# Weighted sum of a windowed attention written transposed with v stationary, probabilities normalised on GpSimd

## The chip, the cores and the metric

The kernel runs on one core of one Trainium2 chip. Its engines each run their own instruction stream and meet at semaphores: TensorE (PE in the rows; PEld is its weight load), VectorE (DVE), ScalarE (ACT), GpSimd (POOL), and SyncE (SP), which here only issues DMAs. The metric is the device time of one execution in microseconds (us). The profiled execution is one run with the hardware profiler on; its rows give times in us from the start of its span, and mean durations in ns.

## What is computed

Four residual steps on x of 4 x 512 x 128 in float32: a gated linear attention, a block of windowed-attention and MLP layers, a state-space (Mamba) layer, and the same windowed block again. Only the two windowed blocks are touched. One of their six layers is, cut to what matters:

```python
def local_attention(q, k, v):            # 16 heads of 64, windows of 32 tokens
    bk2, bv2 = look(bk), look(bv)        # each window sees itself and the one before: 64 keys
    sim = jnp.einsum('bhwie,bhwje->bhwij', bq, bk2) * QK_SCALE
    sim = jnp.where(mask, -jnp.finfo(sim.dtype).max, sim)
    attn = jax.nn.softmax(sim, -1)
    out = jnp.einsum('bhwij,bhwje->bhwie', attn, bv2)
    return out.reshape(b, h, n, d)

for i in range(6):
    x = attn_layer(shift_tokens(x), Wqkv[i], q_scale[i], k_scale[i], Wo[i]) + x
    x = ffn_layer(shift_tokens(x), ln_g[i], ln_b[i], W1[i], b1[i], W2[i], b2[i]) + x
```

attn_layer projects x to q, k and v, normalises and rotates q and k, calls local_attention and multiplies the result by Wo. ffn_layer is a LayerNorm, two up projections, a GELU and a down projection.

## The kernel before

Each windowed block is 24 iterations (6 layers x 4 batches), and each iteration handles the 512 tokens of one batch as four tiles of 128 tokens. The body of tile u (u = 0 to 3, called body u below) is written out by hand on every engine, in pe_body, act_body, dve_body and the loop over pool_rotate, and this hand-written order is the order of the work: no engine leaves it, each waits at its next semaphore. Two blocks of 24 iterations make 48 iterations and 192 bodies. Most iterations run in a hardware loop whose branch stands between body 3 and body 0.

The work is pipelined over tiles. Body u projects tile u+2 (pe_proj, six chunks of 512 columns into two PSUM banks in turn: chunks 0 to 3 are q and k, 4 and 5 are v), transposes q and k of tile u+1 and makes its scores (pe_qk_t, pe_scores), and transposes the probabilities of tile u and multiplies them with v (pe_probs_t, pe_pv). Between these stands a slice of the MLP of the batch before: in body 0 the Wo product (pe_wo, 2 x 8 matmuls), in body 1 the centring and variance (pe_center, pe_var), in body 2 the spread of 1/std (pe_rstd, L393) and the first up projection (pe_up, L405 and L406), in body 3 the other two up projections and the down projection.

PSUM has eight banks: proj_ps (2), tr_ps (2, all transposes), s_ps (2, scores), o_ps (2, weighted sum and MLP). The path of one tile from scores to Wo before the change:

- ScalarE: act_exp_odd (8 activations with sums, L556) and act_exp_even (L563) write the unnormalised probabilities m["p"]. DVE: dve_den sums the even heads (L732) and takes the reciprocal (L736) of all 16 sums.
- TensorE: pe_probs_t (L315) transposes m["p"] into tr_ps, ScalarE copies it out (act_probs_t, L546). pe_pv (L348) then multiplies: for each of 8 head pairs, 2 parities and 4 windows, one matmul with a 64 x 32 block of transposed probabilities as stationary operand and 64 columns of v as moving operand. A float32 matmul is two records in the trace, so a half of pe_pv is 32 matmuls and 64 records. The result stands as tokens x channels in o_ps.
- DVE: dve_out (L743) multiplies o_ps by the reciprocals into m["o"]. One body later TensorE transposes m["o"] (pe_out_t, L285, 8 transposes) into tr_ps, and ScalarE copies it to m["ot"] (act_out_t, L528), from which pe_wo reads.

GpSimd in body u adds the rotated halves of q and k of tile u+2 (L895, one for each of four chunks, each after DVE's product L686), then refines the inverse norms (L882 to L885) and scales the four chunks (L901). ScalarE squares the chunks (L510) and copies v to m["v"] (L518). SyncE then issues 16 DMAs per tile that spread v over m["vp"] (sp_pairs); for tile u+2 they wait until the weighted sum of tile u is done (o_mm), and act_v of the next body waits for them to land.

## Time and profile before

| | us |
|---|---|
| median of 3 runs | 4693.23 |
| lowest, highest | 4692.45, 4695.45 |
| profiled execution | 4693.35 |
| its span, first to last instruction | 4691.5 |

Mean granted TensorE clock in the profiled execution: 0.918 of full speed. The profiled execution lies 0.1 us from the median and 1.9 us above its own span. A busy TensorE is not one at its peak, since matmuls overlap and their ends are modelled; what a group of matmuls costs is therefore read from the distance between the start of the first row and the start of the next one.

### The profile page before, as it was taken

Reading aid. Unit: us, or ns where it says so; the run is one execution under the profiler, and the core shown is the slowest. Engines: PE = TensorE matmul, PEld = TensorE weight load, DVE = VectorE, ACT = ScalarE, POOL = GpSimd, SP = SyncE. Lnnn points to the kernel's source line nnn. Section 1 sums busy time; section 2 is a strip of 40 time slices with the busy share of each in tenths; the row PEclk is TensorE's granted clock in tenths of the full one; section 3 lists DMA queues with packets and bytes.
Section 4 is the critical chain, followed back from the end, with each engine's and each line's share of the span. In section 5 each row is a group of like instructions: output and inputs, shape, how many; then the busy total and the mean of one; then the engine's idle time right before and its main releaser. Section 6 shows DMA issues by size and latency. Waiting matters only on the chain. (4 is left out here: it accounts for less than half of the span.)

```text
span 4691.5 us, 161781 instructions
## 1 busy us (share of the span) xinstructions
PE 3817.1 (81%) x62204; PEld 2454.2 (52%) x62204; DVE 3473.8 (74%) x5422; ACT 2716.9 (58%) x6885; POOL 2274.0 (48%) x2468
## 2 busy tenths in 40 slices
PE   7788888888888888885655688888888888888887
PEld 2465555555555555552111265655656565565654
DVE  7677777777777777764888777777777777777774
ACT  2466566666656666662333366665666666566663
POOL 3455545554555555440444565555555555555551
PEclk9899999999999999996677799999999999999998
DMA  1222222222222222220000022222222222222221
GB/s 33 57 75 74 72 74 68 71 72 73 74 71 74 67 74 70 73 71 13 0 0 0 21 69 72 73 75 69 73 73 70 69 75 74 68 75 72 70 69 47
DMA packets 243984, 290.20 MB, mean 62 GB/s; under 512 B 60750, under 2 KB 131014, under 8 KB 243142
## 3 DMA queue, kind: packets, MB, share of 16 engines
q1 hardware_dynamic: 243262, 279.62, 23.2%
q8 instruction: 569, 9.32, 0.9%
q14 instruction: 153, 1.25, 0.1%
HBM read 77.03 MB, written 1.05 MB: 17 GB/s over the span
## 5 line engine op out<-in xcount | busy, mean ns | idle before, releaser
L895 POOL TENSOR_TENSOR qk_rows<-rot_products 128x512 f32<-128x512 f32 x768 | 982.3, 1279 | 1601.2 <-DVE rot_products L686 1601.2
L686 DVE TENSOR_TENSOR rot_products<-psum,rot_scaled 128x1024 f32<-128x1024 f32 x768 | 936.5, 1219 | 319.4 <-ACT squares L510 270.3
L271 PE MATMUL psum<-wqkv_hi,xs_hi 128*128 (+1 forms) x1152 | 618.7, 537 | 234.7 <-ACT v_rows L518 85.8
L901 POOL TENSOR_TENSOR qk_rows<-qk_rows,rnorm 128x512 f32<-128x512 f32 x768 | 801.7, 1074 | 15.0
L518 ACT ACTIVATE v_rows<-psum 128x512 f32<-128x512 f32 x384 | 223.8, 597 | 899.1 <-PE psum L273 681.6
L299 PE MATMUL psum<-ident,qk_rows 128*128 128x128 f32 x3072 | 508.1, 318 | 240.1 <-issue 152.8
L510 ACT ACTIVATE squares<-psum 128x512 f32<-128x512 f32 x768 | 481.3, 627 | 223.0 <-PE psum L273 187.6
L299 PEld LDWEIGHTS psum<-ident,qk_rows 128*128 128x128 f32 x3072 | 413.0, 163 | 364.1 <-issue 329.4
L688 DVE TENSOR_REDUCE sumsq<-squares 128x8 f32<-128x512 f32 x768 | 519.1, 676 | 0.0
L743 DVE TENSOR_TENSOR o_rows<-psum,rden 128x512 f32<-128x512 f32 x384 | 247.8, 686 | 309.6 <-PE psum L348 304.9
L272 PE MATMUL psum<-wqkv_lo,xs_hi 128*128 (+1 forms) x1152 | 474.2, 412 | 0.0
L273 PE MATMUL psum<-wqkv_hi,xs_lo 128*128 (+1 forms) x1152 | 474.1, 412 | 0.0
L556 ACT ACTIVATE probs<-psum,minus_row_max 128x64 f32<-128x64 f32 x1536 | 458.7, 328 | 13.8 <-DVE minus_row_max L720 12.2
L271 PEld LDWEIGHTS psum<-wqkv_hi,xs_hi 128*128 128x128 f32 x1152 | 233.5, 203 | 350.5 <-issue 302.7
L1410 POOL TENSOR_TENSOR mb_hc<-mb_h,mb_c 128x512 f32<-128x512 f32 x128 | 211.4, 1670 | 354.4 <-DVE mb_h L1379 337.4
L348 PE MATMUL psum<-v_pairs,probs_t 64*32 64x64 f32 x24576 | 355.4, 228 | 27.5 <-issue 20.6
L348 PEld LDWEIGHTS psum<-v_pairs,probs_t 64*32 64x32 f32 x24576 | 279.9, 107 | 180.3 <-issue 179.1
L371 PE MATMUL psum<-o_t,wo 128*128 128x512 f32 x768 | 352.4, 602 | 11.1 <-issue 10.7
L334 PEld LDWEIGHTS psum<-k_t,q_t 64*32 64x32 f32 x24576 | 269.7, 105 | 151.6 <-issue 150.9
L556 ACT ACTIVATION_READ_ACCUMULATOR probs<-psum,minus_row_max 128x1 f32 x1536 | 338.6, 220 | 0.0
L334 PE MATMUL psum<-k_t,q_t 64*32 64x64 f32 x24576 | 332.6, 224 | 2.6 <-issue 2.6
L546 ACT ACTIVATE probs_t<-psum 128x512 f32<-128x512 f32 x384 | 207.2, 594 | 168.1 <-PE psum L315 168.0
(161 smaller groups left out, 6653.4 us busy)
## 6 DMA issues: line engine op xcount, KB each, us to landing
v_pairs<-v_rows SPq DMA_DIRECT2D x3072, 64.0 KB, 2.0
wo<-in_Wo SPq DMA_DIRECT2D x48, 512.0 KB, 4.0
wqkv_staged<-in_Wqkv SPq DMA_DIRECT2D x52, 384.0 KB, 3.2
w<-in_W SPq DMA_DIRECT2D x48, 341.0 KB, 3.1
w<-in_W SPq DMA_DIRECT2D x48, 128.0 KB
w<-in_W SPq DMA_DIRECT2D x48, 42.5 KB
qk_scale<-in_qk_scale SPq DMA_DIRECT2D x12, 128.0 KB, 3.3
rot_base<-in_rot SPq DMA_DIRECT2D x2, 512.0 KB, 3.7
```

Of the source, the lines that this page charges most:

```text
L271: nc.tensor.matmul(proj_ps[c % 2], xh, wh, start=True, stop=False)
L272: nc.tensor.matmul(proj_ps[c % 2], xh, wl, start=False, stop=False)
L273: nc.tensor.matmul(proj_ps[c % 2], xl, wh, start=False, stop=True).then_inc(S["qkv_mm"], 1)
L299: last = nc.tensor.transpose(tr_ps[g % 2][:, i * P:(i + 1) * P], m["qk"][:, u % 2, (4 * g + i) * P:(4 * g + i + 1) * P], ident[:, :])
L334: last = nc.tensor.matmul(s_ps[par][WIN * w:WIN * w + WIN, 64 * hp:64 * hp + 64], m["qt"][rows, hp, WIN * w:WIN * w + WIN], m["kt"][rows, ...
L348: last = nc.tensor.matmul(o_ps[par][WIN * w:WIN * w + WIN, 64 * hp:64 * hp + 64], m["pt"][rows, hp, WIN * w:WIN * w + WIN], m["vp"][rows, ...
L510: nc.scalar.activation(m["sq"][:, c % 2, :], proj_ps[c % 2], ACT.Square).then_inc(S["sq_done"], 1)
L556: last = nc.scalar.activation(m["p"][:, hp, 1, :], s_ps[1][:, 2 * WIN * hp:2 * WIN * (hp + 1)], ACT.Exp, bias=m["mx"][:, 1, hp:hp + 1], ac ...
L686: V.tensor_tensor(m["mm"][:, c % 2, :, :].rearrange("p a (h e) -> p a h e", e=DH), ps, cos_sin, ALU.mult)\
L688: V.tensor_reduce(m["ss"][:, HC * c:HC * c + HC], m["sq"][:, c % 2, :].rearrange("p (h e) -> p h e", e=DH), AX.X, ALU.add)\
L895: G.tensor_tensor(qk[:, c * CH:(c + 1) * CH].rearrange(half, a=2, e=DH // 2), cos, sin[:, :, ::-1, :], ALU.add)\
L901: G.tensor_tensor(part, part, m["rn"][:, u % 2, HC * c:HC * c + HC].unsqueeze(2) .to_broadcast([P, HC, DH]), ALU.mult).then_inc(S["rot_don ...
```

## The change

The matmul of the weighted sum swaps its operands: v (64 x 64) is stationary, the transposed probabilities (32 columns) are moving, and the result comes out as channels x tokens, as pe_wo wants it. The transposes of m["o"] go, with m["o"] itself. A reciprocal belongs to a token and a head, which now lie along the columns of o_ps, so the normalisation moves ahead of the transpose of the probabilities: GpSimd multiplies m["p"] by the reciprocals (pool_probs, two instructions of 128 x 512) after the add of chunk 1, and pe_probs_t waits for it (pn_done). DVE's dve_out goes. ScalarE copies o_ps straight to m["ot"], at the end of body u instead of in the middle of body u+1. The matmuls run over windows, then over two neighbouring head pairs (j, which picks the half of the array's columns), then over parity (which picks the half of its rows); their number stays. Everything that waited for o_ps to be read by DVE (o_ev) now waits for ScalarE's copies (oT_ev). The rows of Wo are permuted on the host to match.

```diff
-        def pe_out_t(it, u, qk_after):
-
-            for g in range(2):
-                nc.tensor.wait_ge(S["o_ev"], cnt(it, 2, u, 2))
-                if qk_after:
-                    nc.tensor.wait_ge(S["qkT_ev"], cnt(it, 4, u + 2, g + 3))
-                else:
-                    nc.tensor.wait_ge(S["pT_ev"], cnt(it, 2, u, g + 1))
-                for i in range(4):
-                    hp = 4 * g + i
-                    last = nc.tensor.transpose(tr_ps[g][:, i * P:(i + 1) * P],
-                                               m["o"][:, hp, :, :].rearrange("p a e -> p (a e)"),
-                                               ident[:, :])
-                last.then_inc(S["oT_mm"], 1)
...
-        def pe_probs_t(it, u, qk_after, out_before):
+        def pe_probs_t(it, u, qk_after):
 
             for g in range(2):
-                nc.tensor.wait_ge(S["exp0_done"], cnt(it, 1, u, 1))
-                nc.tensor.wait_ge(S["exp1_done"], cnt(it, 1, u, 1))
-                if out_before:
-                    nc.tensor.wait_ge(S["oT_ev"], cnt(it, 2, u - 1, g + 1))
-                elif qk_after:
+                nc.tensor.wait_ge(S["pn_done"], cnt(it, 2, u, 2))
+                if qk_after:
                     nc.tensor.wait_ge(S["qkT_ev"], cnt(it, 4, u + 1, g + 3))
+                else:
+                    wait(nc.tensor, S["pT_ev"], cnt(it, 2, u - 1, g + 1))
...
-            for hp in range(4 * half, 4 * half + 4):
-                for par in range(2):
-                    rows = slice(64 * par, 64 * par + 64)
-                    for w in range(WPT):
-                        last = nc.tensor.matmul(
-                            o_ps[par][WIN * w:WIN * w + WIN, 64 * hp:64 * hp + 64],
-                            m["pt"][rows, hp, WIN * w:WIN * w + WIN],
-                            m["vp"][rows, u % 2, w, DH * hp:DH * hp + DH],
-                            start=True, stop=True)
-                    if hp == HP - 1:
-                        last.then_inc(S["o_mm"], 1)
+            for hp in range(4 * half, 4 * half + 4, 2):
+                for w in range(WPT):
+                    for j in range(2):
+                        for par in range(2):
+                            rows = slice(64 * par, 64 * par + 64)
+                            last = nc.tensor.matmul(
+                                o_ps[par][64 * j:64 * j + 64, P * (hp // 2) + WIN * w:P * (hp // 2) + WIN * w + WIN],
+                                m["vp"][rows, u % 2, w, DH * (hp + j):DH * (hp + j) + DH],
+                                m["pt"][rows, hp + j, WIN * w:WIN * w + WIN],
+                                start=True, stop=True)
+                            if half == 1 and hp == 6 and w == WPT - 1 and j == 1:
+                                last.then_inc(S["o_mm"], 1)
...
-            wait(nc.tensor, S["o_ev"], cnt(it, 2, u))
+            wait(nc.tensor, S["oT_ev"], cnt(it, 2, u))
...
-                if prev:
-                    pe_out_t(it, u - 1, nxt)
...
-                pe_probs_t(it, u, nxt, prev)
+                pe_probs_t(it, u, nxt)
...
         def act_out_t(it, u):
             t = u % TILES
+            nc.scalar.wait_ge(S["o_mm"], cnt(it, 2, u, 2))
+            if t == 0:
+                wait(nc.scalar, S["d1_mm"], it + u // TILES)
             for g in range(2):
-                nc.scalar.wait_ge(S["oT_mm"], cnt(it, 2, u, g + 1))
-                if t == 0:
-                    wait(nc.scalar, S["d1_mm"], it + u // TILES)
                 nc.scalar.activation(m["ot"][:, 4 * g:4 * g + 4, t * P:(t + 1) * P],
-                                     tr_ps[g].rearrange("p (i q) -> p i q", i=4), ACT.Copy).then_inc(S["oT_ev"], 1)
+                                     o_ps[g].rearrange("p (i q) -> p i q", i=4), ACT.Copy).then_inc(S["oT_ev"], 1)
...
                     act_square(it, u + 3, 0)
                 if nxt:
                     act_exp_even(it, u + 1)
+                act_out_t(it, u)
...
-        def dve_out(it, u):
-            V.wait_ge(S["den_done"], cnt(it, 1, u, 1))
-            for g in range(2):
-                V.wait_ge(S["o_mm"], cnt(it, 2, u, g + 1))
-                wait(V, S["oT_mm"], cnt(it, 2, u))
-                V.tensor_tensor(m["o"][:, :, g, :], o_ps[g].rearrange("p (h e) -> p h e", e=DH),
-                                m["rden"][:, u % 2, g, :].unsqueeze(2).to_broadcast([P, 8, DH]),
-                                ALU.mult).then_inc(S["o_ev"], 1)
...
+        def pool_probs(it, u):
+            G.wait_ge(S["den_done"], cnt(it, 1, u, 1))
+            for par in range(2):
+                p = m["p"][:, :, par, :]
+                G.tensor_tensor(p, p, m["rden"][:, u % 2, par, :].unsqueeze(2).to_broadcast([P, HP, 2 * WIN]), ALU.mult).then_inc(S["pn_done"], 1)
+
+        def pool_rotate(it, u, norm=False):
             qk = m["qk"][:, u % 2, :]
             wait(G, S["qkT_mm"], cnt(it, 4, u - 1))
...
+                if norm and c == 1:
+                    pool_probs(it, u - 2)
```

Three places show what the edits do to the order. In the first, TensorE in body 2, the rows run from after the second chunk of the projection to the transposes of the probabilities (L285 is pe_out_t, L271 to L273 are one chunk of the projection, L405 and L406 the up projection, L315 the transposes of the probabilities). Before:

```order
L285 MATMUL psum<-ident,o_rows 128x128 [waits qkT_ev,o_ev]
L285 MATMUL psum<-ident,o_rows 128x128 x3
...
L271 MATMUL psum<-wqkv_hi,xs_hi 128x512 [waits m_done,sq_done]
L272 MATMUL psum<-wqkv_lo,xs_hi 128x512
L273 MATMUL psum<-wqkv_hi,xs_lo 128x512
L405 MATMUL psum<-xn_mlp,w 128x512 [waits xn2,w1_in,o_ev]
L406 MATMUL psum<-xn_mlp,w 128x512
L315 MATMUL psum<-ident,probs 128x128 [waits oT_ev,exp1_done,exp0_done]
L315 MATMUL psum<-ident,probs 128x128 x3
```

The same place in the changed kernel:

```order
L270 MATMUL psum<-wqkv_hi,xs_hi 128x512 [waits m_done,sq_done]
L271 MATMUL psum<-wqkv_lo,xs_hi 128x512
L272 MATMUL psum<-wqkv_hi,xs_lo 128x512
L388 MATMUL psum<-xn_mlp,w 128x512 [waits xn2,w1_in,oT_ev]
L389 MATMUL psum<-xn_mlp,w 128x512
L298 MATMUL psum<-ident,probs 128x128 [waits qkT_ev,pn_done]
L298 MATMUL psum<-ident,probs 128x128 x3
```

Eight transposes are gone, and those of the probabilities wait for GpSimd (pn_done) in place of ScalarE's exponentials. The second place is ScalarE from the end of body 1 to the middle of body 2 (L563 is act_exp_even, L539 copies q and k out of tr_ps, L510 squares a chunk, L528 is act_out_t). Before:

```order
L563 ACTIVATE probs<-probs 128x8x64 [waits sub_done]
L539 ACTIVATE q_t<-psum 128x512 [waits qkT_mm,s_mm]
L539 ACTIVATE q_t<-psum 128x512 [waits qkT_mm]
L510 ACTIVATE squares<-psum 128x512 [waits red_done,qkv_mm]
L539 ACTIVATE k_t<-psum 128x4x128 [waits qkT_mm,s_mm]
L539 ACTIVATE k_t<-psum 128x4x128 [waits qkT_mm]
L510 ACTIVATE squares<-psum 128x512 [waits red_done,qkv_mm]
L528 ACTIVATE o_t<-psum 128x4x128 [waits oT_mm] x2
L510 ACTIVATE squares<-psum 128x512 [waits red_done,qkv_mm]
```

The same place in the changed kernel:

```order
L543 ACTIVATE probs<-probs 128x8x64 [waits sub_done]
L508 ACTIVATE o_t<-psum 128x4x128 [waits o_mm]
L508 ACTIVATE o_t<-psum 128x4x128
L519 ACTIVATE q_t<-psum 128x512 [waits qkT_mm,s_mm]
L519 ACTIVATE q_t<-psum 128x512 [waits qkT_mm]
L490 ACTIVATE squares<-psum 128x512 [waits red_done,qkv_mm]
L519 ACTIVATE k_t<-psum 128x4x128 [waits qkT_mm,s_mm]
L519 ACTIVATE k_t<-psum 128x4x128 [waits qkT_mm]
L490 ACTIVATE squares<-psum 128x512 [waits red_done,qkv_mm] x2
```

The two copies to m["ot"] moved ahead of the copies of q. The third place is GpSimd in every body. Before, the four adds of the rotation follow each other:

```order
L895 TENSOR_TENSOR qk_rows<-rot_products 128x512 [waits m_done]
L891 REGISTER_ALU
L895 TENSOR_TENSOR qk_rows<-rot_products 128x512 [waits m_done]
L880 REGISTER_ALU
L882 TENSOR_TENSOR newton_t<-newton_y 128x32 [waits rot_done,seed]
```

In the changed kernel the multiplies stand between the second add and the third:

```order
L869 TENSOR_TENSOR qk_rows<-rot_products 128x512 [waits m_done]
L856 REGISTER_ALU
L859 TENSOR_TENSOR probs<-probs,rden 128x8x64 [waits den_done]
L859 TENSOR_TENSOR probs<-probs,rden 128x8x64
L865 REGISTER_ALU
L869 TENSOR_TENSOR qk_rows<-rot_products 128x512 [waits m_done]
```

GpSimd now waits in its stream for DVE's reciprocals (den_done), with the adds of chunks 2 and 3 queued behind.

## Rows read from the trace of the kernel before

**Rows 1.** The page: busy time and share of the span of each engine.

```profile
PE 3817.1 (81%) x62204; PEld 2454.2 (52%) x62204; DVE 3473.8 (74%) x5422; ACT 2716.9 (58%) x6885; POOL 2274.0 (48%) x2468
```

**Rows 2.** Busy time of the engines in bodies 1, 2, 3, 0: PE, PEld, DVE, ACT, POOL; clock.

```profile
1000.92:1016.30 15.38, 13.84 (x326) 10.62 (x319) 14.10 (x24) 11.77 (x24) 8.57 (x10) 1.00 0.29 71
1016.30:1035.42 19.12, 16.51 (x321) 11.56 (x315) 14.55 (x25) 14.18 (x38) 10.01 (x13) 0.91 0.32 84
1035.42:1060.63 25.21, 18.55 (x327) 11.70 (x323) 18.76 (x30) 16.96 (x51) 12.30 (x15) 1.00 0.20 50
1060.63:1082.99 22.36, 20.97 (x325) 13.80 (x325) 14.30 (x24) 9.51 (x28) 11.40 (x12) 0.92 0.33 85
```

**Rows 3.** TensorE's waits in 1002 to 1330 (four iterations): total us, times, longest.

```profile
PE psum L299 <- issue: 14.5, 4, 3.8
PE psum L299 <- ACT q_t L539: 7.5, 4, 2.3
```

**Rows 4.** ScalarE, timeline of bodies 1, 2: start, us, instruction, [idle before, releaser].

```profile
1013.83 1.09 ACT L518 ACTIVATE v_rows<-psum 128x512 f32<-128x512 f32 x2 [3.10 <-DMA v_pairs<-v_rows]
...
1019.56 1.13 ACT L539 ACTIVATE q_t<-psum 128x512 f32<-128x512 f32 x2
...
1025.24 1.08 ACT L528 ACTIVATE o_t<-psum 128x512 f32<-128x512 f32 x2
```

**Rows 5.** TensorE, timeline of body 2.

```profile
1020.35 1.94 PE L299 MATMUL psum<-ident,qk_rows 128*128 128x128 f32 x8 [2.25 <-ACT q_t L539]
...
1024.47 1.03 PE L285 MATMUL psum<-ident,o_rows 128*128 128x128 f32 x8
1025.26 0.48 PE L271 MATMUL psum<-wqkv_hi,xs_hi 128*128 x1
...
1027.76 1.04 PE L315 MATMUL psum<-ident,probs 128*128 128x128 f32 x8
```

**Rows 6.** DVE, timeline: the reciprocals in bodies 2, 3 and 0.

```profile
1026.05 0.25 DVE L736 RECIPROCAL rden<-den 128x16 f32<-128x16 f32 x1
...
1043.28 0.25 DVE L736 RECIPROCAL rden<-den 128x16 f32<-128x16 f32 x1
...
1066.66 0.25 DVE L736 RECIPROCAL rden<-den 128x16 f32<-128x16 f32 x1
```

**Rows 7.** GpSimd: a group of the page, and the timeline of body 2.

```profile
L895 POOL TENSOR_TENSOR qk_rows<-rot_products 128x512 f32<-128x512 f32 x768 | 982.3, 1279 | 1601.2 <-DVE rot_products L686 1601.2
...
1033.55 4.05 POOL L901 TENSOR_TENSOR qk_rows<-qk_rows,rnorm 128x512 f32<-128x512 f32 x4
```

**Rows 8.** Timeline of body 3, on DVE and TensorE.

```profile
1041.90 0.75 DVE L780 SCALAR_TENSOR_TENSOR hidden<-psum,layer_vectors,gelu 128x512 f32<-128x512 f32 x1 [0.18 <-ACT gelu L588]
...
1042.50 1.12 PE L285 MATMUL psum<-ident,o_rows 128*128 128x128 f32 x8 [1.64 <-ACT k_t L539]
...
1045.87 1.03 PE L315 MATMUL psum<-ident,probs 128*128 128x128 f32 x8
```

**Rows 9.** TensorE, timeline of body 0: first half of Wo, then the probabilities.

```profile
1067.41 3.67 PE L371 MATMUL psum<-o_t,wo 128*128 128x512 f32 x8 [0.22 <-issue]
1070.92 1.04 PE L315 MATMUL psum<-ident,probs 128*128 128x128 f32 x8
```

**Rows 10.** Weight loads by line, and two stretches of TensorE's timeline.

```profile
L348 PEld LDWEIGHTS psum<-v_pairs,probs_t 64*32 64x32 f32 x24576 | 279.9, 107 | 180.3 <-issue 179.1
L371 PEld LDWEIGHTS psum<-o_t,wo 128*128 128x128 f32 x768 | 143.2, 191 | 175.8 <-issue 171.9
...
1006.62 0.95 PE L385 MATMUL psum<-mean,hidden 128*128 128x1 f32 x8
...
1034.63 0.86 PE L348 MATMUL psum<-v_pairs,probs_t 64*32 64x64 f32 x64
```

**Rows 11.** The end of the last iteration: DVE's dve_out, then Wo.

```profile
4637.78 1.29 DVE L743 TENSOR_TENSOR o_rows<-psum,rden 128x512 f32<-128x512 f32 x2 [1.65 <-issue]
...
4641.83 1.19 PE L371 MATMUL psum<-o_t,wo 128*128 128x512 f32 x1 [0.73 <-issue]
```

More of the change, by code:

```diff
@@ L376, in pe_center @@
         def pe_center(e, o_free):
-            wait(nc.tensor, S["o_ev"], o_free)
+            wait(nc.tensor, S["oT_ev"], o_free)
             nc.tensor.wait_ge(S["d1_ev"], e + 1)
@@ L381, in pe_var @@
         def pe_var(e, o_free):
-            wait(nc.tensor, S["o_ev"], o_free)
+            wait(nc.tensor, S["oT_ev"], o_free)
             nc.tensor.wait_ge(S["xc_ev"], 2 * (e + 1))
@@ L389, in pe_rstd @@
         def pe_rstd(e, o_free):
-            wait(nc.tensor, S["o_ev"], o_free)
+            wait(nc.tensor, S["oT_ev"], o_free)
             nc.tensor.wait_ge(S["diag_done"], e + 1)
@@ L396, in pe_up @@
             if j < 2:
-                wait(nc.tensor, S["o_ev"], o_free)
+                wait(nc.tensor, S["oT_ev"], o_free)
             if j == 0:
@@ L494, in pe_ffn @@
             pe_body(last, True, False)
-            pe_out_t(last, 3, False)
             pe_wo(last, 0)
@@ L644, in act_ffn @@
             act_body(last, True, False)
-            act_out_t(last, 3)
             act_center(last)
@@ L827, in dve_body @@
                     dve_rstd(it - 1)
-                dve_out(it, u)
         def dve_weights(it):
@@ L910, in pool_ffn @@
                 for u in range(TILES):
-                    pool_rotate(it, u + 2)
+                    pool_rotate(it, u + 2, True)
             for u in range(2):
-                pool_rotate(last, u + 2)
+                pool_rotate(last, u + 2, True)
+            for u in range(2, TILES):
+                pool_probs(last, u)
         SP = nc.sync
@@ L1570, in layout @@
          "W2": f["L0_ffn_W2"]}
+    heads = [4 * i + 2 * j + par for par in range(2) for i in range(4) for j in range(2)]
+    r["Wo"] = r["Wo"].reshape(DEPTH, HEADS, DH, D)[:, heads].reshape(DEPTH, INNER, D)
     qs, ks = f["L0_ffn_q_scale"], f["L0_ffn_k_scale"]
```

15 lines of the change are left out of this document (5 added, 10 removed).

## Prediction

> **What bounds the kernel now.** Read the shares first. TensorE is busy 81% of the span, DVE 74%, ScalarE 58%, GpSimd 48% [rows 1], and in one iteration of 82.07 us, bodies 1, 2, 3 and 0, TensorE is busy 69.87, the sum of its column [rows 2]. TensorE is the nearest to a bound, but 12 us of an iteration are not its work, so the second view is what it waits for. Its longest waits are 3.6 us at the loop's branch and 1.9 us for ScalarE's copy of q at the start of body 2, each once per iteration [rows 3]. So the kernel changes its bound within one iteration, and I walk through it body by body.
>
> Body 1 hangs on the DMAs of v: ScalarE stands still 3.10 us until they land and only then, at 1013.83, copies v [rows 4]. From there it has no gap: exponentials, a chunk, exponentials, and the copies of q at 1019.56. TensorE, idle since before, gets its bank back at 1020.35 [rows 5]. Those DMAs start when the weighted sum of body 0 is done, so body 1 has about 3 us in which TensorE and GpSimd may be late at no cost. From the probabilities of body 2 on, TensorE paces itself to the end of that body. At the start of body 3 ScalarE is the late one again: its GELU releases DVE at 1041.90, and TensorE waits 1.64 us for the copy of k queued behind that GELU [rows 8]. After the probabilities of body 3, and through body 0, TensorE sets the time.
>
> **The change, part by part.** The profiled execution took 4693.35 us, 0.1 from the median, so the sum is made against 4693.4. Stretches are counted from the start of one row to the start of the next.
>
> *Transposes of the weighted sum.* Eight transposes advance TensorE by 1025.26 - 1024.47 = 0.79 us [rows 5]. That is saved only where TensorE sets the time: in body 0, where also the 0.22 us before Wo go [rows 9], since the copies that Wo needs are then made a body earlier. Together -1.0. In bodies 1, 2 and 3 something else arrives later, as follows.
>
> *ScalarE's copies to m["ot"].* The two copies take 1.08 us [rows 4], before and after, but they move from the middle of a body, where ScalarE often waits, to just ahead of the copies of q. At the end of body 1 ScalarE has no gap, so the copies of q and the transposes of k behind them come 1.1 us later: TensorE's wait of 2.25 us [rows 5] grows. At the end of body 2 it is the same, since ScalarE works without a gap from the copy of v to the GELU [rows 8]: again +1.1. At the end of body 3 the loop's branch (3.6 us) hides it, at the end of body 0 the 3 us of body 1 do.
>
> *DVE's dve_out.* Two instructions less per body. DVE only waits longer for ScalarE's squares instead, so nothing is gained on the path. Should DVE have been the late one, up to 1.3 us per body would come back.
>
> *GpSimd's multiplies.* No row has this form. The nearest are the scaling by rnorm, 4.05 us for four, 1.01 each, and the rotation's add with a reversed operand, 1.28 [rows 7]. I take 1.05, as the scaling is the same operation with the same broadcast: 2.1 us a body (2.0 to 2.6). They start when the reciprocals are there and TensorE follows. A handover between engines shows as 0.18 us [rows 8]; I count 0.3 for both. GpSimd has the time: it is busy at most 12.30 us of any body [rows 2]. The question is when they end, against TensorE's present start of the transposes of the probabilities:
> - Body 2: reciprocals end at 1026.30 [rows 6], multiplies at 1028.4, TensorE could start at 1028.7. It starts at 1027.76 now [rows 5]. So +0.9, on top of the 1.1 by which this whole chain is already late.
> - Body 3: 1043.53 [rows 6] + 2.4 = 1045.9 against 1045.87 [rows 8]: nothing beyond the 1.1. The 1.64 us and the 0.79 us that TensorE saves here are used up in waiting.
> - Body 0: 1066.91 [rows 6] + 2.4 = 1069.3 against 1070.92 - 1.0 = 1069.9 [rows 9]: hidden, with 0.6 us to spare.
> - Body 1: late by 1 to 2 us, hidden by the wait for the DMAs.
>
> Behind the waiting multiplies stand the adds of chunks 2 and 3. They wait for DVE's third product anyway, which comes only after the reciprocals, so they lose under a microsecond, and GpSimd's next wait, for DVE's seeds of the inverse norms, takes it up.
>
> *The weighted sum itself.* Still 64 records per half, 0.86 us now [rows 10]. The moving side halves from 64 to 32 columns; the stationary side doubles from 32 to 64. A load of 32 columns lasts 107 ns, one of 128 columns 191 [rows 10], so a column costs 0.88 ns and 64 columns occupy their part of the array for 56 ns. The variance stretch shows what a stream looks like that is bound by loads: 8 loads of 128 columns in 0.95 us, some 0.1 each [rows 10]. Today's 64 loads of 32 columns would take 64 x 28 ns = 1.8 us one after another, and the half takes 0.86, so at least two to three of them run at once. After the change there are four independent quarters. If all four load at once, a half needs 64 x 56 / 4 = 0.9 us plus the last matmul: I take +0.2 per half. If only 2.5 do, 1.4 us, +0.6. Below: if streaming alone set the pace, half the columns could save up to 0.2 per half. So +0.4 per body (-0.4 to +1.2). It counts in bodies 3 and 0, +0.8; in body 2 ScalarE's 1.1 cover it up to 1.1, in body 1 the DMAs do.
>
> The Trainium skill has a rule against this very swap. TensorEngine Tiling (Array Packing), section Instruction Overhead: each matmul carries some 60 cycles, one of 1 column takes as long as one of 60, and a tiling factor should not be taken from a dimension that is already small. By it 64 records of 32 columns cannot pass faster than 25 ns apart, 1.6 us a half, and the time would be near 4940 (+1.5 per body: 2 x 1.5 in bodies 3 and 0 and 0.4 in body 2, on 2.1 from the other terms). By the rows the sum keeps its +0.2: they have 64 records of 64 columns in 0.86 us, 13 ns apart, already below that floor.
>
> *Sum.* Per iteration 1.1 + 0.9 + 1.1 - 1.0 + 0.8 = +2.9 us. Two iterations of the 48 are first ones without MLP, so 46 x 2.9 = +133. At the end of a block the change helps: from dve_out at 4637.78 to Wo at 4641.83 are 4.05 us [rows 11], of which only ScalarE's two copies and a handover, about 1.4, remain. Twice -2.6 is -5. 4693.4 + 133 - 5 = **4821 us**, slower by 2.7%. With the ends of the weighted sum (-0.8 and -0.8 more, or +1.6 and a little) this case spans 1.3 to 4.7 us per iteration: 4748 to 4905.
>
> **The rivals.**
> - *The late waits are hidden, and TensorE's work decides.* Then each body saves 0.79 and pays 0.4, body 3 loses its 1.64 and body 0 its 0.22: -3.4 per iteration, 48 x 3.4 = 163, **4530 us**. For it: TensorE is the busiest engine. It decides if the reciprocals of bodies 2 and 3 come more than 2 us earlier than now, say because DVE without dve_out is ahead. Against it: the squares and the copies of q, not DVE, gate them. 0.12.
> - *The weight loads bind.* Two to three at once: 1.4 us per half, +4.7 per iteration, **4904 us**. It shows as a half of more than 1.2 us. For it: nothing in the rows shows four loads at once with certainty. The skill's rule above ends here too. 0.15.
> - *The clock.* In bodies 2 and 0, which start with TensorE's long waits, the granted clock is 0.91 and 0.92 on average, in the other two it is 1.00 [rows 2]. The change adds idle stretches of 1 to 2 us ahead of the probabilities in bodies 1, 2 and 3. If one of them per iteration brings a further stretch at 1.2 instead of 2.4 GHz of the kind that body 2 has now (9% of 19.12 us, doubled: 3.4 us at half speed, 1.7 lost), that is +1.7 per iteration, **4899 us**. Against it: the 1.64 us wait in body 3 leaves that body at 1.00. 0.13.
> - *Both effects are half as large* and the result is within 0.2% of now: 0.05.
>
> **How the numbers follow.** My case 0.55, faster 0.12, loads 0.15, clock 0.13, no change 0.05. The likeliest is my case, 4821 us. The range must leave out at most 0.2: it drops the faster rival and the ends, and takes 4730 to 4930. Slower by over 0.2% (about what a measurement of this kernel tells from none): 0.55 + 0.15 + 0.13 = 0.83; same 0.05; faster 0.12.
>
> **What would show it.** Right: TensorE's wait for the copy of q in body 2 grows from 2.25 to about 3.3 us; the probabilities' transposes wait for GpSimd in bodies 1, 2 and 3, and not in body 0; the idle before the projection's chunk 0 in body 1 stays bound to the DMAs; a half of the weighted sum lasts 1.0 to 1.1 us. Wrong: no wait for GpSimd in body 2 (then the first rival), a half at or below 0.86 us, an iteration under 82 us, or a mean clock well under 0.918.

## The result, and the profile after

| | before | after |
|---|---|---|
| median, us (lowest to highest of 4 runs) | 4694.34 (4692.45 to 4695.82) | 5002.71 (5002.20 to 5005.41) |
| ratio to before, 95% interval | | 1.0658 (1.0640 to 1.0677) |
| profiled execution: time, span, us | 4693.35, 4691.5 | 5002.95, 5000.5 |

The change makes the kernel 6.6% slower. The forecast was 2.7% slower, 4821 us, with a range to 4930: the sign was right, and of the loss of 308 us it had 128. The span and mean granted clock of after:

```profile
core 0: 5000.5 us, clock 0.892
```

Its page, busy time and share of each engine:

```profile
PE 3891.9 (78%) x60668; PEld 2452.9 (49%) x60668; DVE 3390.9 (68%) x5038; ACT 2736.1 (55%) x6885; POOL 2676.2 (54%) x2852
```

Against [rows 1], GpSimd has 402 us more, DVE 83 us less, ScalarE 19 us more. TensorE has 1536 matmuls less and is busy 75 us *longer*: at a clock of 0.892 instead of 0.918 it spends more time at 1.2 GHz. So the loss is in waits and in clock, not in work. TensorE's waits of after from 1002 to 1330, four iterations (line waited at, releaser: total us, times, longest), the answer to [rows 3]:

```profile
PE psum L283 <- issue: 17.0, 4, 4.9
PE psum L298 <- POOL probs L859: 9.6, 11, 1.4
PE psum L388 <- ACT o_t L508: 6.9, 4, 1.8
PE psum L283 <- ACT q_t L519: 6.3, 3, 2.1
...
PE psum L271 <- issue: 3.5, 4, 1.2
```

L283 is the transpose of q and k (L299 before), L298 that of the probabilities (L315), L388 the first projection of the MLP, L271 a part of the projection. Three waits of weight are new. That for GpSimd's probabilities comes in bodies 1, 2 and 3 (1.39, 1.01 and 0.34 us in the timeline; 11 times in the four iterations) and not in body 0, as forecast. That of L388 for ScalarE's copies, 1.7 us per iteration, I had not listed. And behind the branch stands a second wait for nothing but the next instruction, up to 1.2 us here. One wait of before is gone, the one in which TensorE stood in body 1 until ScalarE had copied v (same view of the kernel before):

```profile
PE psum L271 <- ACT v_rows L518: 7.0, 4, 2.3
```

It stood late in body 1 (1.43 us at 1014.63) and was part of that body's slack.

Three groups of the page of after: GpSimd's multiplies, then loads and matmuls of the weighted sum (busy us, mean ns, idle before):

```profile
L859 POOL TENSOR_TENSOR probs<-probs,rden 128x512 f32<-128x512 f32 x384 | 401.3, 1066 | 199.9 <-DVE rden L714 199.9
...
L332 PEld LDWEIGHTS psum<-probs_t,v_pairs 64*64 64x64 f32 x24576 | 403.0, 136 | 155.2 <-issue 154.3
...
L332 PE MATMUL psum<-probs_t,v_pairs 64*64 64x32 f32 x24576 | 447.6, 221 | 14.3 <-issue 10.1
```

A multiply takes 1.07 us (forecast 1.05). A load of 64 columns is recorded with 136 ns where one of 32 had 107 [rows 10]. How the bodies follow each other now, in one iteration of after (bodies 1, 2, 3), from the timelines of TensorE, ScalarE and GpSimd in order of time:

```profile
1071.38 2.09 POOL L859 TENSOR_TENSOR probs<-probs,rden 128x512 f32<-128x512 f32 x2 [0.18 <-DVE rden L714]
1073.53 1.95 PE L298 MATMUL psum<-ident,probs 128*128 128x128 f32 x8 [1.39 <-POOL probs L859]
1079.88 0.60 ACT L498 ACTIVATE v_rows<-psum 128x512 f32<-128x512 f32 x1 [1.15 <-PE psum L272]
1085.12 1.13 ACT L508 ACTIVATE o_t<-psum 128x512 f32<-128x512 f32 x2
1086.08 1.15 ACT L519 ACTIVATE q_t<-psum 128x512 f32<-128x512 f32 x2
1086.89 1.62 PE L283 MATMUL psum<-ident,qk_rows 128*128 128x128 f32 x8 [1.97 <-ACT q_t L519]
1092.67 2.09 POOL L859 TENSOR_TENSOR probs<-probs,rden 128x512 f32<-128x512 f32 x2 [2.35 <-DVE rden L714]
1094.81 1.10 PE L298 MATMUL psum<-ident,probs 128*128 128x128 f32 x8 [1.01 <-POOL probs L859]
1099.97 1.14 PE L332 MATMUL psum<-probs_t,v_pairs 64*64 64x32 f32 x64
1106.58 1.12 PE L388 MATMUL psum<-xn_mlp,w 128*128 128x512 f32 x2 [1.77 <-ACT o_t L508]
```

Body 1 starts late: GpSimd ends its multiplies at 1073.47, TensorE then transposes the probabilities at half speed (1.95 us for 8 instead of 1.04) and, a few steps on, ScalarE's copy of v waits for TensorE, where before it waited for the DMAs [rows 4]. Then ScalarE's two copies stand ahead of those of q, 0.96 us from start to start. And the branch and the start of body 0 of after, on TensorE:

```profile
1035.92 1.13 PE L332 MATMUL psum<-probs_t,v_pairs 64*64 64x32 f32 x64
1040.47 1.97 PE L283 MATMUL psum<-ident,qk_rows 128*128 128x128 f32 x8 [3.42 <-issue]
1042.09 0.78 PE L270 MATMUL psum<-wqkv_hi,xs_hi 128*128 x1
1043.67 0.79 PE L271 MATMUL psum<-wqkv_lo,xs_hi 128*128 x1 [0.80 <-issue]
...
1048.52 0.63 PE L272 MATMUL psum<-wqkv_hi,xs_lo 128*128 x1
1048.95 3.97 PE L354 MATMUL psum<-o_t,wo 128*128 128x512 f32 x8
```

From the branch until Wo everything runs at half speed: a matmul of a chunk takes 0.63 to 0.79 us instead of 0.39 to 0.50, and even Wo takes 3.97 instead of 3.67 [rows 9]. These rows hold the part that the forecast lacked: the longer stretch at 1.2 GHz, and the 0.80 us of a second stop.

### The profile page after: what moved, and what is told of

Same layout as the page of the kernel before. It is cut to its first block and busy times, and to the rows that moved or that the text cites. A ratio compares the mean times of both kernels' runs of the same rounds, so it can differ in the third digit from the quotient of the medians.

```text
span 5000.5 us, 157822 instructions
## 1 busy us (share of the span) xinstructions
PE 3891.9 (78%) x60668; PEld 2452.9 (49%) x60668; DVE 3390.9 (68%) x5038; ACT 2736.1 (55%) x6885; POOL 2676.2 (54%) x2852
## 3 DMA queue, kind: packets, MB, share of 16 engines
q8 instruction: 596, 9.76, 0.9%
HBM read 77.03 MB, written 1.05 MB: 16 GB/s over the span
## 5 line engine op out<-in xcount | busy, mean ns | idle before, releaser
L283 PE MATMUL psum<-ident,qk_rows 128*128 128x128 f32 x3072 | 503.9, 315 | 344.5 <-issue 224.5
L270 PE MATMUL psum<-wqkv_hi,xs_hi 128*128 (+1 forms) x1152 | 630.1, 547 | 147.5 <-DVE x_ffn L723 50.0
L283 PEld LDWEIGHTS psum<-ident,qk_rows 128*128 128x128 f32 x3072 | 408.3, 161 | 452.5 <-issue 436.0
L859 POOL TENSOR_TENSOR probs<-probs,rden 128x512 f32<-128x512 f32 x384 | 401.3, 1066 | 199.9 <-DVE rden L714 199.9
L271 PE MATMUL psum<-wqkv_lo,xs_hi 128*128 (+1 forms) x1152 | 488.8, 424 | 17.2 <-issue 17.2
L272 PE MATMUL psum<-wqkv_hi,xs_lo 128*128 (+1 forms) x1152 | 483.9, 420 | 0.0
L332 PEld LDWEIGHTS psum<-probs_t,v_pairs 64*64 64x64 f32 x24576 | 403.0, 136 | 155.2 <-issue 154.3
L332 PE MATMUL psum<-probs_t,v_pairs 64*64 64x32 f32 x24576 | 447.6, 221 | 14.3 <-issue 10.1
L317 PEld LDWEIGHTS psum<-k_t,q_t 64*32 64x32 f32 x24576 | 282.6, 111 | 166.4 <-issue 166.2
L317 PE MATMUL psum<-k_t,q_t 64*32 64x64 f32 x24576 | 348.5, 236 | 3.2 <-issue 3.1
L298 PE MATMUL psum<-ident,probs 128*128 128x128 f32 x1536 | 235.9, 303 | 146.8 <-POOL probs L859 146.8
```

Source lines behind the costliest of these rows:

```text
L270: nc.tensor.matmul(proj_ps[c % 2], xh, wh, start=True, stop=False)
L271: nc.tensor.matmul(proj_ps[c % 2], xh, wl, start=False, stop=False)
L272: nc.tensor.matmul(proj_ps[c % 2], xl, wh, start=False, stop=True).then_inc(S["qkv_mm"], 1)
L283: last = nc.tensor.transpose(tr_ps[g % 2][:, i * P:(i + 1) * P], m["qk"][:, u % 2, (4 * g + i) * P:(4 * g + i + 1) * P], ident[:, :])
L317: last = nc.tensor.matmul(s_ps[par][WIN * w:WIN * w + WIN, 64 * hp:64 * hp + 64], m["qt"][rows, hp, WIN * w:WIN * w + WIN], m["kt"][rows, ...
L332: last = nc.tensor.matmul(o_ps[par][64 * j:64 * j + 64, P * (hp // 2) + WIN * w:P * (hp // 2) + WIN * w + WIN], m["vp"][rows, u % 2, w, DH ...
```

## The experiments

Each time is a median of 4 runs (6 for e4, 10 for e8, e9, e12, e13 and e17), beside runs of the kernel before on the same chip (4692 to 4697 us). They came in this order: first the parts of the change one by one, then idle work put into the gaps, and then, when these did not add up, the place of the code.

**The parts, in the kernel as it was changed.** e1_no_norm leaves the multiplies out (and with them the normalisation):

```diff
-                nc.tensor.wait_ge(S["pn_done"], cnt(it, 2, u, 2))
+                nc.tensor.wait_ge(S["exp0_done"], cnt(it, 1, u, 1))
+                nc.tensor.wait_ge(S["exp1_done"], cnt(it, 1, u, 1))
...
-                if norm and c == 1:
-                    pool_probs(it, u - 2)
```

> The changed kernel without GpSimd's two multiplies per tile; TensorE's transposes of the probabilities wait for the exponentials again. Leaves out: the softmax normalisation. Theory S (the schedule alone: waits, copies and weight loads as forecast, 2.9 us per iteration): only body 2's 0.9 us comes back, 46 x 0.9 = 41, so about 4960. Theory C (the clock: 3.7 of the 6.6 us per iteration are TensorE at half speed, entered after idle stretches): the half-speed stretch that begins before the probabilities of body 1 goes too, another 1.2 to 1.4 us per iteration, so about 4900, and the half-speed stretch at the start of body 0 stays.

Measured 4862.87 us, ratio 1.0357 (1.0333 to 1.0380).

e2_dve_copy gives the copies to m["ot"] to DVE, where dve_out stood:

```diff
-                act_out_t(it, u)
...
+                V.tensor_copy(m["ot"][:, 4 * g:4 * g + 4, t * P:(t + 1) * P],
+                              o_ps[g].rearrange("p (i q) -> p i q", i=4)).then_inc(S["oT_ev"], 1)
...
+                dve_out_t(it, u)
```

> The changed kernel with the copies to m["ot"] made by DVE at the place of the old dve_out, not by ScalarE. Theory S: ScalarE's 1.1 us at the start of body 2 and again in body 3 go, 46 x 2.2 = 101, so about 4900, and the first up projection of body 3 no longer waits for copies (1.8 us each iteration in the trace). Theory C says the same of these, but leaves the half-speed stretch of 10.2 us at the start of body 0, unless the copies are what causes it: then 2.7 us more per iteration, about 4780.

Measured 4860.24, ratio 1.0346 (1.0326 to 1.0367).

e4_swap_alone is the kernel before with nothing but the new pe_pv; the layout of what it computes no longer fits what follows:

```diff
-                            m["pt"][rows, hp, WIN * w:WIN * w + WIN],
-                            m["vp"][rows, u % 2, w, DH * hp:DH * hp + DH],
+                                m["vp"][rows, u % 2, w, DH * (hp + j):DH * (hp + j) + DH],
+                                m["pt"][rows, hp + j, WIN * w:WIN * w + WIN],
```

> The kernel before with one thing changed: the matmuls of the weighted sum take v as the stationary operand and write channels x tokens, as in the changed kernel. All else stays, so DVE scales and TensorE transposes the wrong way round. Leaves out: a right layout of the weighted sum. Both theories: a half lasts 1.14 us instead of 0.86, 0.56 us per body, which counts in bodies 3 and 0 at least: +1.1 us per iteration, +52, about 4746. Theory S with all four bodies counting: +2.2, 4797. If the mean clock falls from 0.918 as well, the swap itself has a share in the clock (theory C2).

Measured 4712.33, ratio 1.0041 (1.0028 to 1.0055). So the swap of the operands costs 18 us, half of what the forecast gave it, and 290 of the 308 us are elsewhere.

e7_dve_both puts both on DVE: the copies as in e2, the multiplies right behind the reciprocals.

```diff
+            V.wait_ge(S["den_done"], cnt(it, 1, u, 1))
+            for par in range(2):
+                p = m["p"][:, :, par, :]
+                V.tensor_tensor(p, p, m["rden"][:, u % 2, par, :].unsqueeze(2).to_broadcast([P, HP, 2 * WIN]),
+                                ALU.mult).then_inc(S["pn_done"], 1)
```

> The changed kernel with both moved steps on DVE: the copies to m["ot"] at the place of dve_out, and the normalisation of the probabilities right behind the reciprocals (two instructions on SBUF, some 0.7 us each). Against the run with DVE's copies alone (4860): the normalised probabilities come about 1 us sooner (1.4 against 2.1 us and no handover to GpSimd), in bodies 1, 2 and 3. Theory S: 1.0 us in body 2 and some of it in body 3, 46 x 1.5 = 69, so 4790. Theory C adds the half-speed stretch before body 1's probabilities (160 us in all, 80 lost) if the wait shrinks enough: 4710.

Measured 4796.40, ratio 1.0221 (1.0204 to 1.0238). Undoing both new engine steps returns 206 us and still leaves 103 us over the kernel before. The swap accounts for 18 of them; 85 are explained by neither.

**Idle matmuls in TensorE's gaps**, results unused, to keep its clock up. e5_fill_branch has 14 of them, of 512 columns, behind body 3's last weighted sum; e8_before_fill and e9_both_fill are the same in the kernel before and in e7; e6_fill_probs has 6 ahead of the wait for GpSimd in bodies 1 and 2.

```diff
                pe_pv(it, u, 1)
+                if u == 3 and ahead:
+                    pe_fill(14)
...
+                if ahead and u in (1, 2):
+                    nc.tensor.wait_ge(S["qkT_ev"], cnt(it, 4, u + 1, 4))
+                    pe_fill(6)
                pe_probs_t(it, u, nxt)
```

> The changed kernel with 14 idle matmuls (bfloat16, 512 columns, some 3.0 us together, result never read) behind the last weighted sum of body 3, to be worked off while TensorE's sequencer goes round the loop. Theory C: body 0 no longer runs its first 10 us at 1.2 GHz, which cost 2.7 us more than before per iteration: about 4870, mean clock up from 0.892 to 0.93 or more. Theory S: nothing is gained, and what of the 3.0 us isn't hidden is added: 5000 to 5140.

Measured 4858.12, ratio 1.0356 (1.0336 to 1.0375), clock 0.925.

> The changed kernel with 6 idle matmuls (bfloat16, 512 columns, some 1.3 us, result never read) ahead of TensorE's wait for the normalised probabilities, in bodies 1 and 2, where TensorE waited 1.0 to 1.4 us for GpSimd. Nothing gets ready sooner by it. Theory C: the half-speed stretches that begin between the probabilities of body 0 and of body 1 (140 us of them in all) go, at half of that per iteration 1.5 us, so about 4930. Theory S: no change, 5003, or slower by what of the fill sticks out.

Measured 4883.96, ratio 1.0401 (1.0383 to 1.0419), clock 0.907.

> The kernel before with the 14 idle matmuls behind the last weighted sum of body 3. It had 208 us at half speed that began between the probabilities of body 3 and of body 0. Theory C: half of that comes back, 104 us, so about 4590, and the mean clock rises from 0.918 to about 0.96. If the fill only helps the changed kernel, 4694.

Measured 4691.79, ratio 0.9997 (0.9975 to 1.0018).

> Both moved steps on DVE and the 14 idle matmuls at the branch: the change with its late waits and its half-speed stretch both attacked. If nothing but these made it slow, TensorE's saving of 0.8 us of transposes per body shows at last and it beats the kernel before with the same fill (4590): 4540 to 4580. If ScalarE and the DMAs of v hold bodies 1 to 3 whatever TensorE does, it ends level with it, 4590 to 4620.

Measured 4675.51, ratio 0.9959 (0.9942 to 0.9975).

Taken at face value, a fill at the branch is worth 145 us to the changed kernel, one before the probabilities 119, and the first is worth nothing to the kernel before. Two fills in different places that gain nearly the same, and in e6 at a place where the waits sum to only a few us per iteration, don't fit a theory of the clock. Both also lengthen the loop, which moves its code.

**The place of the code.** e10_pad24 and e11_pad72 are the changed kernel with 24 or 72 one-column matmuls once ahead of each of TensorE's two loops. They run 2 x 24 or 2 x 72 times in 4.9 ms; within the loop nothing changes.

```diff
+            pe_pad(24)
             with nc.tensor.Fori(max(first + 1, 2), last) as it:
                 pe_body(it, True, True)
```

> The changed kernel with 24 idle matmuls of one column ahead of TensorE's loop, executed once per block (about 1 us each time). They move the loop's instructions in memory and nothing else. Theory P (place): the waits named issue behind the loop's branch (4.7 us to the first transposes, then a second one in the projection, 0.8 to 1.2 us) depend on where the loop's code lies, and the half-speed stretch on these waits; in the run with matmuls ahead of the probabilities they had shrunk to 3.7 us and none, and the stretch to Wo from 8.6 to 6.4 us. Then about 3 us per iteration come back: 4860. Theory C (the clock follows from the late work alone): no change, 5003.

Measured 4889.33, ratio 1.0405 (1.0388 to 1.0423).

> As the one before with 72 such matmuls. Theory P: another place, another result, anywhere from 4860 to 5010, but not both times 5003. Theory C: 5003 again.

Measured 4904.11, ratio 1.0433 (1.0416 to 1.0451).

> The kernel before with the 24 idle matmuls of one column ahead of TensorE's loop. Theory P: its time moves too, by up to 3 us per iteration either way, 4590 to 4830. If before's place is as good as any: 4694 to 4700.

Measured 4704.67, ratio 1.0017 (1.0005 to 1.0030).

> Copies and normalisation on DVE, with the 24 idle matmuls of one column ahead of the loop. Without them 4796, with 4.46 us of wait behind the branch and 8.4 us from there to Wo. Theory P: 46 x 3 = 138 less, about 4660, faster than the kernel before. Theory C: 4796.

Measured 4706.02, ratio 1.0020 (1.0009 to 1.0031), 90 us less than e7.

> The changed kernel with 128 idle one-column matmuls ahead of TensorE's loop, once in each of its two loop programs. If the place of the loop's code within a fetched packet of 16 KB decides, 128 pairs of load and matmul move it by one whole packet and the time is that of the changed kernel again, 4985 to 5010 us, with a second wait for issue (some 1 us) in the branch's neighbourhood. If the padding itself (whatever it separates or warms) took the time away in e10 and e11, it stays at 4885 to 4910.

Measured 4994.52, ratio 1.0638 (1.0620 to 1.0655). The time is back, within 8 us of the changed kernel. A little padding takes 113 us away, much padding gives it back, so padding is no cure in itself: it is where the loop's code lies relative to a grid of 128 pairs of load and matmul. The DMA queue that carries instructions (packets, MB, share) moves the code in cells of that size: its packets are 16384 bytes each (9.76 MB in 596). After, e10_pad24 and e14_pad128 in turn:

```profile
q8 instruction: 596, 9.76, 0.9%
```

```profile
q8 instruction: 567, 9.29, 0.8%
```

```profile
q8 instruction: 600, 9.83, 0.9%
```

The Trainium skill, Advanced Engine Details and Errata, section ISA Cache, says that a cache line of 16 KB holds 256 instructions, which is 128 pairs; e14's return agrees. Counted in the trace, an iteration of the hardware loop fetches 12 packets in e10; in after it fetches 13 in 30 of the 41 passes over the branch, and 12 in the other 11. What that costs stands in the groups of TensorE's transposes of q and k and of the chunk's second matmul (the last column is idle time by releaser). After:

```profile
L283 PE MATMUL psum<-ident,qk_rows 128*128 128x128 f32 x3072 | 503.9, 315 | 344.5 <-issue 224.5 <-ACT q_t L519 119.2 <-POOL qk_rows L877 0.7
...
L271 PE MATMUL psum<-wqkv_lo,xs_hi 128*128 (+1 forms) x1152 | 488.8, 424 | 17.2 <-issue 17.2
```

e10_pad24:

```profile
L283 PE MATMUL psum<-ident,qk_rows 128*128 128x128 f32 x3072 | 497.6, 314 | 292.7 <-issue 163.9 <-ACT q_t L524 128.1 <-POOL qk_rows L882 0.5
...
L271 PE MATMUL psum<-wqkv_lo,xs_hi 128*128 (+1 forms) x1152 | 478.9, 416 | 0.0
```

That is 60.6 + 17.2 = 78 us of waiting for the next instruction. Most of it, 65 us, is a second stop some 3 us behind the first. After has it in every one of its 41 passes over the branch, 20 times at L271 and 21 times within the transposes of q and k, for 0.4 to 2.7 us; e10 has it in none. The rest is clock. From the end of body 3's weighted sum to Wo's first matmul, summed over 46 iterations, are 567.8 us in after and 456.4 in e10: the 111 us between them are the whole difference of the two kernels. Some waits for other engines shrink in these stretches, so that all waits together take 74 us of the 111, and 38 are left (111.4 - 73.7) as the price of the longer stretch at 1.2 GHz: 399 of the 568 us were at that clock, against 239 of the 456 (mean clock of the whole span 0.892 and 0.905). The start of body 0 in e10, to be held against the rows of after above; full speed is back at 1031.90, 4.5 us after the start of the first transposes instead of over 8:

```profile
1027.37 1.97 PE L283 MATMUL psum<-ident,qk_rows 128*128 128x128 f32 x8 [4.65 <-issue]
...
1030.41 1.73 PE L283 MATMUL psum<-ident,qk_rows 128*128 128x128 f32 x8
1031.90 0.48 PE L270 MATMUL psum<-wqkv_hi,xs_hi 128*128 x1
...
1033.72 3.60 PE L354 MATMUL psum<-o_t,wo 128*128 128x512 f32 x8
```

**Is the kernel before only lucky?** e17_before_pad64 pads it by half a packet:

> The kernel before with 64 idle one-column matmuls ahead of TensorE's loop. If the kernel before only happened to lie in a good place (24 gave +0.2%), a shift by 8 KB, half a packet, may bring the slow place: 4760 to 4810. If it is indifferent: 4690 to 4710.

Measured 4701.35, ratio 1.0019 (1.0009 to 1.0029). It too fetches more there (590 packets, e12 589, against 569). The group of its transposes of q and k, and that of the chunk's third matmul:

```profile
L299 PE MATMUL psum<-ident,qk_rows 128*128 128x128 f32 x3072 | 498.3, 313 | 262.1 <-issue 153.4 <-ACT q_t L544 97.2 <-POOL qk_rows L906 9.9
L273 PE MATMUL psum<-wqkv_hi,xs_lo 128*128 (+1 forms) x1152 | 476.9, 414 | 8.8 <-issue 8.8
```

and the first of the two in the kernel before:

```profile
L299 PE MATMUL psum<-ident,qk_rows 128*128 128x128 f32 x3072 | 508.1, 318 | 240.1 <-issue 152.8 <-ACT q_t L539 80.7 <-POOL qk_rows L901 4.6
```

So extra packets come in both kernels, and their price is some 9 us in one and over 100 in the other. The traces show the difference: e17 has the second stop behind the branch in 16 passes of 41, 8.8 us in all, and e12 in none, while after, e14, e1, e2 and e7 all have it in all 41, 60 to 70 us in all, ahead of matmuls that then run at 1.2 GHz. e1, e2 and e7 fetch 589, 594 and 598 packets, so their times hold this price too; of the changed kernel's runs so far only e5, e6 and e9, with 567, and the padded e10, e11 and e13 do not. Why the stop falls there in the changed loop at two of the four places tried (0 and 128, not 24 and 72), and hardly in the loop of before at any of three, is not settled; I have no run on that.

**The parts again, with the loop in the good place.** e15_no_norm_pad24, e16_dve_copy_pad24 and e18_dve_norm_pad24 are e1, e2 and the DVE multiplies of e7 alone, each with the 24 of padding.

> The changed kernel without GpSimd's multiplies (the normalisation is left out) and with 24 idle one-column matmuls ahead of the loop. Against e10_pad24 (4889) it is the price of the multiplies with the loop in the good place. My theory: only +0.9 in body 2 and 0.5 in body 1 hang on them, 1.4 x 46 = 65 us, so 4825. The rival that the 20 us which the weighted sum costs and ScalarE's copies are all that is left gives 4770.

Measured 4757.94, ratio 1.0136 (1.0119 to 1.0154): the multiplies cost 131 us, twice what this expectation had.

> The changed kernel with the copies to the transposed rows made by DVE, at the place of the old dve_out, and 24 idle one-column matmuls ahead of the loop. Against e10_pad24 (4889) it is the price of ScalarE's copies. Theory of the prediction: 1.1 us in body 2 and 1.1 in body 3, together 2.2 x 46 = 100 us, so 4790. If the copies of q are only part of what gates and DVE's own lateness takes half back: 4840.

Measured 4756.42, ratio 1.0138 (1.0121 to 1.0155): 133 us, more than both.

> The changed kernel with the normalisation on DVE, right behind the reciprocals, ScalarE's copies as in the changed kernel, and 24 idle one-column matmuls ahead of the loop. If the two prices add (GpSimd's multiplies alone cost 4756 - 4706 = 50 us), this gives 4889 - 50 = 4839. If they lie on one chain, where the first of them uses up TensorE's slack and the second is paid in full, each alone is cheap: 4745 to 4765.

Measured 4825.83, ratio 1.0288 (1.0271 to 1.0305): the prices add. With e10 and e13 this makes a square; e15 stands beside it. Medians in us, and under them the median distances between the starts of the probabilities' transposes, body 0 to 1, 1 to 2, 2 to 3 and 3 to 0, over the full iterations of each trace (before: 18.62, 19.58, 18.11, 25.22):

| | no normalisation | normalisation on DVE | on GpSimd |
|---|---|---|---|
| copies on DVE | not run | 4706.0 (19.57, 18.53, 18.10, 25.24) | 4756.4 (20.35, 19.35, 17.99, 24.95) |
| copies on ScalarE | 4757.9 (19.26, 20.28, 18.41, 24.85) | 4825.8 (19.93, 19.47, 19.06, 25.50) | 4889.3 (20.78, 20.72, 18.98, 25.04) |

Against multiplies on DVE, GpSimd's cost 50 us in the upper row and 63 in the lower, all of it ahead of bodies 1 and 2 (0.8 each in the upper row, 0.9 and 1.3 in the lower), none ahead of body 3. Against no multiplies at all they cost 131, of which 68 remain when DVE makes them; of these 131, 1.5 us per iteration lie ahead of body 1. ScalarE's copies cost 120 and 133 against copies on DVE: 0.9 to 1.4 ahead of body 2, 1.0 ahead of body 3, 0.4 ahead of body 1. In body 3 the wait of L388 goes with the copies. TensorE's waits from 1002 to 1330 in e18:

```profile
PE psum L388 <- ACT o_t L513: 6.3, 4, 1.7
...
PE psum L298 <- DVE probs L723: 2.8, 8, 0.5
```

and in e16:

```profile
PE psum L298 <- POOL probs L873: 11.5, 12, 1.5
PE psum L388 <- DVE hidden L762: 4.6, 4, 1.3
```

**The fill again.** e19_before_fill_pad118 is e8 with its loop moved by ten pairs less than a packet.

> The kernel before with 14 idle matmuls of 512 columns at the end of body 3 and 118 pairs of padding ahead of TensorE's loop, ten less than one packet of 16 KB. If the fill keeps TensorE's clock up as it does in the changed kernel and only the place of the code took it away in e8 (4691.8), this gives 4655 to 4675. If the kernel before has no use for the fill, 4690.

Measured 4656.89, ratio 0.9929 (0.9907 to 0.9951), clock 0.935, 575 packets where e8 had 601. So e8 had gained and lost at once. Priced in the good place, the fill brings 4889 - 4858 = 31 us to the changed kernel (e5 lies well by its own length: 567 packets), 31 to e13 (e9), and 38 to the kernel before (one padded run of it, e19); e6's brings 5. In e19 the branch is passed like this, TensorE's timeline:

```profile
1051.75 3.19 PE L431 MATMUL psum<-maskrow,onehot 64*128 64x512 bf16 x14
1055.35 1.09 PE L299 MATMUL psum<-ident,qk_rows 128*128 128x128 f32 x8 [0.40 <-issue]
1056.19 0.48 PE L271 MATMUL psum<-wqkv_hi,xs_hi 128*128 x1
```

The idle matmuls cover the branch, which takes as long as ever (3.5 us from the weighted sum's end at 1051.82), and the first transposes and the chunk behind them run at 2.4 GHz. This is the best kernel of the study, 0.7% faster than before; the best one with the idea of the change is e9, 19 us behind.

## Why the prediction was wrong

The 182 us between 4821 and 5002.7 fall in two parts. The step that put the time out of the range is the first, a term that the sum had at nothing: with the loop in the good place the same change measures 4889.3, within 4730 to 4930.

**1. A term that was not there: 113 us.** The sum had nothing for where the loop's code lies, that is, for instruction fetch. It listed TensorE's longest wait, 3.6 us for issue at the branch [rows 3], and treated it as fixed, only as cover for ScalarE's copies. The change takes 32 transposes with their loads out of the loop and so moves every line of it; e10 and e14 show that the place, not the missing work, costs 5002.7 - 4889.3. The clock rival had the right symptom (a further stretch at 1.2 GHz), but for this part the wrong cause and place: it blamed the waits ahead of the probabilities, and these 113 us lie behind the branch. Its own place is not cleared. In e10 the stretches at 1.2 GHz between the probabilities of body 1 and of body 2 sum to 227 us, against 137 before, which is at most 45 us of TensorE's work within the 196 below. e6's fill gained 5 us but left 202 of the 227 as they were, so it doesn't tell what they cost.

**2. The sum itself: 68 us short.** In the good place the change costs 4889.3 - 4693.4 = 196 us, 4.3 per iteration, where the sum had 2.8. The terms below overlap and are held against different kernels, so they do not add up to the 196 us. By its terms:

- *ScalarE's copies*, forecast 1.1 in each of bodies 2 and 3: measured 2.6 to 2.9 (120 to 133 us) against copies on DVE. Mechanism right, the size low by 0.4 to 0.7, mostly for the part ahead of body 1, which had been priced at nothing. In body 3 it acts through L388, whose bank is now freed by the copies, not through the copy of k that I named.
- *GpSimd's multiplies*, forecast 0.9, all in body 2: measured 2.9 (131 us, e10 against e15) against none at all, as the forecast priced them. This is the term furthest off. Making them on GpSimd and not on DVE is 1.1 to 1.4 of it (50 to 63 us). 1.05 us per multiply was right (two in 2.09 us), and body 0 at nothing was nearly right (0.2). In body 3 the place on GpSimd costs nothing beyond DVE, though against no multiplies 0.6 remain. Body 1, 1.5 us, was priced at nothing. All else of the change together costs 66 us in e15, 1.4 per iteration, where the sum had 2.0.
- *Body 1 at no cost* is the step that failed in this part. The forecast left 3 us of cover by the DMAs and let 1 to 2 us of lateness vanish in it. But the second chunk of v that ScalarE copies comes from TensorE behind the late probabilities, and it becomes the last to arrive: the row of after at 1079.88 waits for TensorE's L272 where [rows 4] waited for a DMA. It waits for TensorE in 43 of 44 iterations of after and 31 of 44 of e10, and in none of before or of e15. Counted from the end of body 0's weighted sum, the probabilities of body 1 start at 6.4 us before and 8.36 in e10, that copy at 13.88 and 14.50, the copy of q at 19.12 and 20.69 (medians). Of 1.95 us of lateness 0.6 get through; with ScalarE's 0.96, q is 1.6 late.
- *The weighted sum*, +0.2 per half: measured 0.28 (1.14 against 0.86). By the forecast's estimate 64 loads of 64 columns at 56 ns, four at once, are 0.9 us plus the last matmul: that choice fits, and the rival in which loads bind (a half over 1.2 us) falls. The whole swap costs 18 us in e4, where the sum had 37: in body 3 part of it is covered, since TensorE's wait behind it, at the branch, sums to 141 us in e4 and 153 before.
- *The transposes' saving*, -1.0: not isolated. e13, with the swap, without transposes and with every other step on DVE, is 9 us above before instead of 28 below (18 - 46), but DVE's multiplies, on its path then, are in it too. This stays open.
- *The Trainium skill's rule*, TensorEngine Tiling (Array Packing), section Instruction Overhead: by it a half would have taken 1.6 us and the time been near 4940. The trace does not agree: the half took 1.14, and e4 puts the whole swap at 18 us. 4940 would have been nearer to 5002.7 than 4821 by luck, for a reason that isn't there.

The tail was as forecast: from the last weighted sum's end to Wo only ScalarE's copies remain, 1.3 us. In after, last iteration, timelines of ScalarE and TensorE, to be held against [rows 11]:

```profile
4951.20 1.08 ACT L508 ACTIVATE o_t<-psum 128x512 f32<-128x512 f32 x2 [7.22 <-PE psum L332]
...
4952.43 1.10 PE L354 MATMUL psum<-o_t,wo 128*128 128x512 f32 x2 [1.30 <-ACT o_t L508]
```

The forecast of the wait for q in body 2 (2.25 to 3.3 us) was wrong as a sign to look for: it stands at 1.97, because TensorE is now late as well. Two engines that are late by like amounts show no longer wait between them.

## What to carry to other kernels

When a trace shows that a hardware loop fetches its code anew in each iteration (here 12 packets), any edit may move the code against the fetch grid: repeat the measurement with some idle instructions ahead of the loop before an edit of a few per cent is believed or explained, and compare the page's count of instruction packets and the waits for issue behind the branch. The count alone is no price (589 packets cost 8 us in e12, 596 cost 113 in after). Prices of parts are best taken between kernels with the same count and the same stops. A step that is hung between two engines can be paid twice, once for its own time where it stands ahead of something due and once more where the lateness outlasts its cover: follow each cover to the last of the things it waits for, not to the one that was last before.

## What the runs showed of the hardware

- TensorE stands still for 3.2 to 5.0 us at its loop's branch in each iteration of after, for 3.4 to 4.2 before; idle matmuls ahead of it cover this and don't shorten it (e19: 3.5 us from the weighted sum's end to the first transpose).
- The changed loop took 2.3% less time by a shift of its code by 24 pairs of instructions (5002.7 to 4889.3 us), 2.0% less by 72, and 0.2% less by 128; the loop before only 0.2% more by 24 or 64.
- The slow places show a second stop of 0.4 to 2.9 us behind the branch in all 41 passes, 60 to 70 us in all; the good ones of the changed loop show none over 0.2 us.
- Matmuls of four quarters of the array, 64 rows by 64 columns each, pass at 1.14 us for 64 with a new load each and 32 columns moving, 18 ns apart. With 32 columns stationary and 64 moving it is 0.86 us, 13 ns.
- GpSimd scales 128x512 f32 by a broadcast operand in 1.07 us by the group's mean, 2.09 us for two in a row; the like operation of [rows 7] takes four in 4.05 us.
